# First graph attention layer of a two-layer kernel: weight turns and sums moved one pipeline step nearer to their scores

## The reference

```python
Q, K, V = (enh @ W + b).reshape(N, H, D)          # H = 4 heads, D = 64
mod_k = K[src] + 0.2 * rel[:, None, :]            # rel = rel_w[edge_relations]
scores = einsum('ehd,ehd->eh', Q[dst], mod_k) / D ** 0.5
ex = exp(scores - segment_max(scores, dst)[dst])
w = ex / segment_sum(ex, dst)[dst]
agg = segment_sum(w[:, :, None] * V[src], dst)    # then Wo, + x, layer norm
```

## Time and profile before

| | us |
|---|---|
| median of three runs | 4821.75 |
| profiled execution | 4847.24 |
| its span | 4845.9 |
| TensorE busy | 4004.0 (83%) |
| VectorE busy | 3436.6 (71%) |
| GpSimd busy | 3127.0 (65%) |
| ScalarE busy | 2781.9 (57%) |

### The profile page before, as it was taken

How to read it: one execution, slowest core, us unless ns; L and a number is a source line. 1 busy time by engine, 2 the same in 40 slices (tenths; PEclk the granted TensorE clock), 3 DMA queues, 4 the chain that set the end, 5 groups by cost and what they waited for, 6 DMA issues and landing times. The chain is left out here.

```text
span 4845.9 us, 149801 instructions
## 1 busy us (share of the span) xinstructions
PE 4004.0 (83%) x42462; PEld 2592.5 (53%) x42462; DVE 3436.6 (71%) x11602; ACT 2781.9 (57%) x7985; POOL 3127.0 (65%) x3229
## 2 busy tenths in 40 slices
PE   6978889889998888988889688777788777777785
PEld 4645545555555555555555456555565555555553
DVE  3235667677777777777777568888887787777887
ACT  2324444445454455445545367777777777777775
POOL 1226666666666666666666277777777777777773
PEclk9989999999999999999999677877767887888776
DMA  6878888888888888888888377777777777777774
GB/s 207 282 225 232 236 224 226 231 236 234 235 243 231 234 240 241 231 240 239 232 237 237 101 193 208 206 207 206 208 208 205 207 207 204 204 203 206 205 205 131
DMA packets 820558, 1052.06 MB, mean 217 GB/s; under 512 B 458633, under 2 KB 632338, under 8 KB 820464
## 3 DMA queue, kind: packets, MB, share of 16 engines
q0 software_dynamic: 225072, 726.83, 51.5%
q1 hardware_dynamic: 594078, 323.35, 26.7%
q10 hardware_dynamic: 1314, 0.99, 0.1%
HBM read 915.79 MB, written 133.39 MB: 217 GB/s over the span
## 5 line engine op out<-in xcount | busy, mean ns | idle before, releaser
L765 POOL DMA_INDIRECT typed_rows<-kv,typed_index x1563 | 1491.3, 954 | 857.4 <-PE typed_p_o L889 420.3
L1288 POOL DMA_INDIRECT plain_rows<-xp,plain_index x1563 | 1563.2, 1000 | 556.3 <-issue 437.2
L1140 ACT ACTIVATE typed_far<-typed_match,all_cst 128x416 bf16<-128x416 uint8 x521 | 334.2, 642 | 1002.2 <-DVE typed_col L991 983.8
L1393 PE MATMUL plain_p_o<-plain_rows,plain_weight_t 128*64 128x130 f32 (+1 forms) x8336 | 864.3, 350 | 49.5 <-DVE plain_weight_t L1419 48.8
L1380 PE MATMUL plain_p_s<-all_cst,plain_rows 128*128 128x128 f32 (+1 forms) x2084 | 453.9, 317 | 362.0 <-DMA plain_rows<-xp,plain_index 360.2
L1393 PEld LDWEIGHTS plain_p_o<-plain_rows,plain_weight_t 128*64 128x64 f32 (+1 forms) x8336 | 574.2, 170 | 212.0 <-issue 131.7
L851 PE MATMUL typed_p_kt<-all_cst,typed_rows 128*128 128x128 f32 x3126 | 473.8, 290 | 255.8 <-DMA typed_rows<-kv,typed_index 254.9
L964 DVE TENSOR_TENSOR typed_kt<-typed_p_kt,typed_rel 128x768 f32<-128x768 f32 x521 | 497.0, 954 | 230.7 <-PE typed_p_kt L851 202.2
L1380 PEld LDWEIGHTS plain_p_s<-all_cst,plain_rows 128*128 128x128 f32 (+1 forms) x2084 | 334.9, 173 | 515.1 <-issue 497.4
L851 PEld LDWEIGHTS typed_p_kt<-all_cst,typed_rows 128*128 128x128 f32 x3126 | 345.1, 145 | 359.1 <-DMA typed_rows<-kv,typed_index 299.0
L1426 DVE CUSTOM_DVE_ANT_0 plain_alpha<-plain_alpha,plain_far 128x416 f32<-128x416 f32 x521 | 310.6, 596 | 313.1 <-ACT plain_alpha L1542 299.9
(11 more groups left out here) (190 smaller groups left out, 6341.7 us busy)
## 6 DMA issues: line engine op xcount, KB each, us to landing
typed_match<-match SPq DMA_DIRECT2D x131, 208.0 KB
plain_match<-match SPq DMA_DIRECT2D x131, 208.0 KB
agg<-qkv_zero SPq DMA_DIRECT2D x98, 264.0 KB
typed_agg<-agg SPq DMA_DIRECT2D x98, 264.0 KB
plain_agg<-agg SPq DMA_DIRECT2D x98, 264.0 KB
kv<-qkv_kv SPq DMA_DIRECT2D x98, 258.0 KB
typed_kinds<-match SPq DMA_DIRECT2D x131, 192.0 KB
typed_rows<-kv,typed_index POOLq DMA_INDIRECT x1563
```

Source lines behind the costliest of these rows:

```text
L765: pool.indirect_dma_start(rows[:, r, j, :], None, k.kv, bass.IndirectOffsetOnAxis(ap=index[:, g, at:at + 1], axis=0)).then_inc(rows_in[r], 16)
L1140: act.activation(far[:], match[:, slab, t.slot(TPB)], ACT.Square, bias=cst[:, C_CODE:C_CODE + 1], scale=FAR).then_inc(far_ready, 1)
L1288: pool.indirect_dma_start(rows[:, r, j, :], None, k.xp, bass.IndirectOffsetOnAxis(ap=index[:, g, at:at + 1], axis=0)).then_inc(rows_in[r], 16)
L1393: last = pe.matmul(p_o[at:at + HC, t.slot(2), 0:2 * V], weight_t[0:e, t.slot(2), j * P + at:j * P + at + HC], val[:, 2 * V * g:2 * V * g + ...
```

## The change

Three things, all in `attend_typed`. The lag of the weight turns goes from 5 to 4 and that of the sums from 6 to 5 (scores stay at 3), with the output queue's lag from 8 to 7. TensorE's step becomes relate(t), score(t-3), aggregate(t-5), arrive(t-1), turn_weights(t-4). VectorE's step becomes lower_bound(s-5), prepare(s), add_keys(s-3), copy_weights(s-6), block parts; ScalarE's step becomes message copy, relations, weigh, put, set_apart, copy_weights, block parts. No instruction is added or taken out, and buffers and waits keep their form.

```diff
-    R, M, KEY, SCORE, TURN_LAG, LAG = 8, 4, 1, 3, 5, 6
+    R, M, KEY, SCORE, TURN_LAG, LAG = 8, 4, 1, 3, 4, 5
...
-            interleave(sp, FIRST, TilePart(8, put_out), TilePart(0, fetch), BlockPart(0, 0, load), BlockPart(6, 10, store))
+            interleave(sp, FIRST, TilePart(7, put_out), TilePart(0, fetch), BlockPart(0, 0, load), BlockPart(6, 10, store))
...
-            parts = (TilePart(0, relate), TilePart(KEY, arrive), TilePart(TURN_LAG, turn_weights), TilePart(SCORE, score))
-
             def step(t, copied=None):
-                for part in parts:
+                for part in (TilePart(0, relate), TilePart(SCORE, score), TilePart(LAG, lambda b: aggregate(b, copied)),
+                             TilePart(KEY, arrive), TilePart(TURN_LAG, turn_weights)):
                     part.at(t)
-                TilePart(LAG, lambda b: aggregate(b, copied)).at(t)
...
-            interleave(v, FIRST, TilePart(KEY + 2, add_keys), TilePart(TURN_LAG + 2, copy_weights), TilePart(0, prepare), TilePart(SCORE + 2, lower_bound),
+            interleave(v, FIRST, TilePart(SCORE + 2, lower_bound), TilePart(0, prepare), TilePart(KEY + 2, add_keys), TilePart(TURN_LAG + 2, copy_weights),
...
-            interleave(act, FIRST, BlockPart(2, 1, copy_message), TilePart(1, copy_relations), TilePart(TURN_LAG + 1, copy_weights), TilePart(SCORE, set_apart), TilePart(SCORE + 1, weigh), TilePart(LAG + 1, put),
+            interleave(act, FIRST, BlockPart(2, 1, copy_message), TilePart(1, copy_relations), TilePart(SCORE + 1, weigh), TilePart(LAG + 1, put), TilePart(SCORE, set_apart), TilePart(TURN_LAG + 1, copy_weights),
```

## The result

The changed kernel takes 4665.69 us (median of four runs, 4660.43 to 4671.13) against 4822.91 for the kernel before: a ratio of 0.9675, 95% interval 0.9658 to 0.9691. That is 157 us less. The forecast was 4700, 123 us less, with a range of 4600 to 4830.

What follows compares the result with a forecast made beforehand. TensorE bounds it: 3.78 us of work in a 4.45 us tile, plus 0.48 waiting for rows. Forecast: 66.1 us in 16 tiles, 4.22 a tile with 0.06 rest and 0.03 rows, hence 4700 us; range 4600 to 4830.

Steps and rivals of the forecast that it cites:

- The rows: First layer's attention: four steps between slot release and key transposes remove TensorE's 0.48 us a tile wait for gathered rows.
- the 9.3 us: Time a tile's gathers need for issue and landing, more than two free-running steps offered before the change.
- The key loop: Key transposes, VectorE's key addition, scores and sums form a 3.63 us loop, 0.30 over TensorE's step, in 13 of 16 steps.
- VectorE's heavy steps: Weight copies on VectorE meet normalisations or joins: 4.05 us a step, 0.42 over 3.63, costing 1.7 us in 16 tiles.
- The sign given for it: GpSimd's wait for an aggregation to free a slot of `rows`, 420.3 us before, grows or stays.
- ScalarE: Its weight copy, now due before the next step's sums, costs nothing: 1.4 us of a 3.63 us step is free.
- The sum: First layer's attention stage: 4.13 us a tile, 4.22 with rest and rows, saving 120 us plus 3 for the drain.
- The rule against the change: Brief TensorE waits between matmul groups swing its clock between two levels, so 0.3 us waits could cost more than long ones.
- The rival built on it: TensorE's clock falls to the next stage's 0.77: 4.7 us a tile, 130 us more, 4950 us; chance 0.12.
- late rows: Rows stay late through DMA bursts; half the wait stays and eats the gain, 4800 to 4820 us; chance 0.13.
- costly score loop: Heavy VectorE steps delay lower bound and next addition without fading: 0.2 us a tile more, 4800 us; chance 0.07.
- free keys: VectorE's key addition overlaps so TensorE never waits: 3.95 to 4.0 us a tile, 4560 to 4590 us; chance 0.13.

Runs made afterwards that it cites:

- the two lead runs: Changed kernel with each gather held back one tile more (three steps of lead): 4662.98 us; two tiles more (two steps): 4838.3 us.
- The keys-first kernel: Changed kernel with TensorE's key transposes before scores, weight transposes last, and VectorE's key addition first: 4600.91 us; on a slow chip 6086.15 us.

## Why the prediction was right, step by step

*The rows.* Right. Three steps of lead cost nothing, two bring the wait back to 0.29 us a tile. I kept 0.03 us a tile; it was 0.01. But the 9.3 us were one late tile's. Counted in the same way the tile before it took 7.4, from 0.30 ahead of its first gather to its key transposes:

```profile
1498.03 0.94 POOL L765 DMA_INDIRECT typed_rows<-kv,typed_index  x1 [2.06 <-PE typed_p_o L889]
...
1505.16 0.87 PE L851 MATMUL typed_p_kt<-all_cst,typed_rows 128*128 128x128 f32 x6 [0.49 <-DMA typed_rows<-kv,typed_index]
```

So two steps, 8.8 us in the run with two steps of lead, are too short for some tiles and not for all; there TensorE waited for rows 160 times in 520 tiles.

*The key loop.* Right in kind and size. Steps without an update last 3.77 us on average against 3.76, and lengthening the addition by 0.31 us costs what 13 steps in 16 say. The wait itself is 198 us in 423 steps, 0.47 each; the forecast had 0.30 and 1.7 / 13 = 0.13 for the heavy steps, 0.43. TensorE's own step shrank by 0.10: with the weight transposes ahead of the relations (1506.75 to 1507.19, 0.44 us) instead of the scores (0.53 in the earlier trace rows) it is 3.23 us (0.52 + 0.84 + 0.72 + 0.71 + 0.44). The loop doesn't care, so a step without an update gained nothing by it; one with an update lasts 5.64 us and not 5.75, 0.02 us a tile.

*VectorE's heavy steps.* Right in total, and partly by luck. 1.7 us in 16 tiles was 0.11 a tile, and the run without VectorE copies gained 0.09. But the forecast had 4 heavy steps of 4.05 us and 9 light ones of 3.63 in 16 tiles. Measured were 6 of 3.97 (192 in the stage) and 7 of 3.60 (230). More heavy steps, each of them and each light one shorter: 48.9 us foreseen, some 49.0 measured.

*GpSimd.* The sign given for it was wrong. Its wait for the sums was to grow or stay and fell from 420 to 177 us. The forecast's own figures ruled growth out: a tile of 4.22 us less 3.75 for its three gathers leaves 0.47, 244 us in the stage. The sum didn't use the sign.

*ScalarE.* Costed at nothing, and no long wait of TensorE for its copies stands in the waits; only weight loads wait for them, 87.5 us, under the matmuls before.

*The sum.* 13 x 3.63 + 3 x 5.75 + 1.7 = 66.1 us in 16 tiles; measured 16 x 4.11 = 65.8. The term that was mis-sized is the rest. I kept 0.06 of the 0.19 us that no term of the kernel before explained, and 0.03 for rows: 4.22. Next to nothing of either was left, and 0.02 came off the steps with an update: 0.11 x 520 = 57 us. What the 0.19 was can be estimated. A granted clock of 0.96 in 2316 us is some 185 us at half clock; at the prediction's factor of 1.75 that costs 185 - 185 / 1.75 = 79 us, 0.15 a tile. The trace puts this behind long waits: 44 of the stage's 52 stretches at half clock begin within 2 us of the end of a wait of over 1.1 us, of which there were 119. Now no wait of the stage is over 0.9 us, the clock is 1.00, and this part is gone. No run changed the clock alone, so it stays an estimate. Part of the 57 us was hidden in the median: I scaled by 0.995, as the profiled execution of before lay 25 us above its median, and that of after lies only 5 above, which takes 19 us off again. 157 against 123 is what remains. The forecast's own range, 4640 to 4760, holds 4665.69; the wide one, to 4830, would have held no change at all too.

*The rule against the change.* Short waits at nearly every step's scores, none over 0.9 us, left the clock at 1.00 in this stage. The Trainium skill, page "TensorE: Matmul & The Clock Gate", section "A second HAM failure mode: psum-queue depth-cycling", tells of another kernel in which brief idling between groups of matmuls makes it swing; this trace doesn't bear that out for waits of this kind. In the second layer's stage, with TensorE busy 1517 of 1950 us, the clock is 0.76, and it was 0.77 before. The rival built on it, 4950 us, didn't happen. Of the other rivals, late rows and costly score loop are out by the two lead runs and the measured step, and free keys by the wait at the scores.

## What to carry to other kernels

When an engine waits for gathered data while the gather queue waits for that engine to free a buffer, count the steps between release and use and compare them with issue plus landing: here the third step of lead was worth all of it, and the fourth nothing. An order that gives the lead also moves other hand-overs; lay out one step with start-to-start times, and look for pairs that now stand side by side, since the same lead with the keys a step ahead was 65 us better. The comparison holds on the chips that take some 4820 us for the kernel before; on those that take over 6000, every order but one ended within 1% of it. Before comparing two kernels, run the same old kernel beside both.

## What the runs showed of the hardware that I had not expected

Chips differ. Two of those that ran these kernels took 6082 and 6027 us for a kernel that takes 4818 to 4824 elsewhere. The keys-first kernel ran on both kinds. On the faster chip its stretch is

```profile
361.00:2436.00 2075.00, 2009.55 (x28240) 1180.48 (x28240) 1627.25 (x4567) 1111.28 (x2848) 1490.69 (x1557) 1.00 0.91 262
```

On the slow one it is 37% longer, 2843 us, with VectorE and GpSimd busy for nearly the same time (1650 and 1487 us). It is tempting to read 191 GB/s against 262 as slow transfers. But the rate is the bytes divided by the time, and both stretches move the same 542 MB. The DMA engines are busy 0.71 x 2843 = 2019 us against 0.91 x 2075 = 1888, 7% more, which is far from 37. TensorE's waits ahead of the key transposes carry the label "issue" there (89.7 us), which could hide late rows. But it stands still ahead of instructions of many other kinds too, even ahead of the second matmul of the relations (line 843), in front of which the program waits for nothing:

```profile
PE typed_p_r L843 <- issue: 41.8, 80, 1.2
```

On the faster chip this row is missing: TensorE's matmuls never wait at that line. So the slow chips aren't shown to be slow in their transfers; what holds the engines up there stays open.

TensorE's step depends on the order of its parts with no wait in it: 3.33 us in the kernel before, 3.23 in the changed one, 3.38 with keys first.
